# Block biases of a graph network leave the matmuls: one becomes a column, two are added to rows in SBUF by transfers from memory

## Chip, core and metric

One core of a Trainium2 chip. The time is that of one execution on the device in microseconds (us), and less is better. TensorE does the matrix products, VectorE and ScalarE take their results out of PSUM, GpSimd computes on SBUF alone, SyncE (SP) issues transfers. ScalarE and GpSimd can issue transfers too.

## What is computed

Four graph layers run over 512 nodes with 512 features, each `x = x + layer(relu(norm(x)))`, all in float32. The change touches mainly the second, a transformer of four blocks with attention along the edges (4 heads of 128):

```
for i in range(4):
    y = cond_norm(x, s1[i], b1[i])
    q, k, v = y @ wq[i] + bq[i], y @ wk[i] + bk[i], y @ wv[i] + bv[i]
    # per head: softmax of q.k over a node's edges, then the sum of p * v[dst]
    x = x + attention(q, k, v) @ wo[i] + bo[i]
    y = cond_norm(x, s2[i], b2[i])
    x = x + relu(y @ m_w1[i] + m_b1[i]) @ m_w2[i] + m_b2[i]
```

The first layer is a normalised adjacency product with two weights and biases, the third three diffusion steps, the fourth two relational layers of the form `agg + x @ root + bias`.

## The kernel before

Every product is made of three float32r matmuls, high by high, high by low and low by high part, so that a tile of 128 rows by 512 columns over 512 summed values takes 12 matmuls. A bias is a 13th matmul of the same shape: a selector (`sel`) times a tensor `brow` that holds the high and the low part of each bias in two rows. A tile goes to one of seven banks of PSUM (`ring`) in an order written out by hand (`l1_order`). ScalarE evicts the high part (`high`, L795), VectorE the low part (`low`, L1155, or L1157 with a column or a scalar). A bank is free again once the semaphore `tile_taken` has counted its eviction.

One block on TensorE (`attention_block`, L2013): transposes "Ta" of the normed rows `yp`; four tiles v; q and k per head; scores "s"; transposed probabilities "PT"; the mean value "PV" of a head, as columns `oT`; four tiles o = oT x wo, the first two begun before the last head is done; each o is added to the residual rows `xl` by VectorE (`residual`, L1544), which then takes the norm's statistics (`norm_stats`). GpSimd computes the inverse root (`inverse_root`, L695), VectorE the two halves of the conditioned norm (`conditioned`, L1487 and L1492) with two more tiles S and B. Transposes "Tb", the hidden tiles M, the tiles X, each added to `xl` again. Between X tiles the norm of the next block begins ("Sa", "Ba", then "Ta" 0).

Weights: ScalarE issues the load of a weight of 1 MB into one of three slots (L765) when the last user of the slot is done, rounds it to its high part (`high_weight`, L770), and GpSimd subtracts to get the low part (`low_weight`, L686). In a block the six weights are wv, wq, wk, wo, m_w1, m_w2 (j = 0 to 5; j = 6 is wv of the next block). GpSimd takes its work in the order of `block_lows` (L733): the splits of j = 1 to 4, four roots, the splits 5 and 6, four roots. ScalarE issues the load of j = 6 behind the eviction of the last "Tb" transpose.

SP loads `quad`, groups of the fourth layer's basis of 960 KB each, all through the kernel; TensorE mixes them (L1773) into a bank of their own. SP also loads the rows of the conditioning, the norms' biases (`load_cond`) and, once per block, the biases bv, bo, m_b1 and m_b2 into `braw` (`load_biases`); VectorE splits them into `brow` (`split_biases`) at the start of a block.

Of the kernel before, what the change touches and what calls it, by code (L numbers as in the profile page):

```python
# [14 lines left out]
P = 128  # L15
# [20 lines left out]
VECS = 5  # L36
COLUMN_BIASES = ("bq", "bk")
# [6 lines left out]
BASES = 30  # L44
VEC_ROWS = (VECS + len(COLUMN_BIASES) * BLOCKS) * KT

# [62 lines left out]
def program(nc, x_d, src_d, dst_d, type_d, w_d, noise_d, l0, l1, l2, l3, out_d, mix_d, ct_d, x_s):  # L109

    top = ExitStack()
    with top:
# [76 lines left out]
        bias_columns = sb("bias_columns", [P, len(COLUMN_BIASES), BLOCKS * KT])  # L189
        gate_e = mask[0:2, 0, :]  # L190
# [19 lines left out]
        braw = sb("braw", [P, D], ctx=cg)  # L210
        brow = sb("brow", [P, D], F32R, ctx=cg)
# [183 lines left out]
        braw_loaded = sem("braw_loaded")  # L395
        brow_hi = sem("brow_hi")
        brow_ready = sem("brow_ready")
# [71 lines left out]
        def _(sp):  # L469
# [25 lines left out]
            small(vec_rows[(VECS - 1) * KT:VECS * KT, :], l0["b_gcn"][0, :].rearrange("(k p) -> k p", p=P))  # L495
# [3 lines left out]
            vecs = [l0["b_mlp"][0:1], l0["b_gcn"][1:2], l0["b_mlp"][1:2]]  # L499
            vecs += [b.rearrange("(a d) -> a d", a=1) for b in (l2["b"], l3["bias"][0], l3["bias"][1])]  # L500
            for j, v in zip((0, 2, 3, 4, 5, 6), vecs):
                small(bias_raw[2 * j:2 * j + 2, :], v.broadcast_to([2, D]))
# [10 lines left out]
            def load_cond(b, n, ready):  # L513
                if ready is not None:
                    sp.wait_ge(cond_ready, ready)
                for k in range(2):
                    w_, b_ = l1[("s", "b")[k] + f"{n + 1}_w"], l1[("s", "b")[k] + f"{n + 1}_b"]
                    for g in range(3):
                        sp.dma_start(craw[32 * g:32 * g + COND, k, :],
                                     w_[bass.ds(b, 1)].rearrange("a c d -> (a c) d")).then_inc(cond_loaded, 16)  # L520
                    sp.dma_start(craw[96:98, k, :], b_[bass.ds(b, 1)].broadcast_to([2, D])).then_inc(cond_loaded, 16)

# [21 lines left out]
            def load_biases(i):  # L544
                for j, name in ((0, "bv"), (3, "bo"), (4, "m_b1"), (5, "m_b2")):
                    sp.dma_start(braw[2 * j:2 * j + 2, :], l1[name][bass.ds(i, 1)].broadcast_to([2, D])
                                 ).then_inc(braw_loaded, 16)

# [18 lines left out]
            load_biases(0)  # L567
# [4 lines left out]
            def block_loads(i, nxt, last):  # L572
# [8 lines left out]
                if not last:  # L581
                    sp.wait_ge(brow_ready, i + 1)
                    load_biases(nxt)
# [28 lines left out]
            store_set(SETS - 1)  # L612
            for t in range(NT):
# [6 lines left out]
        def _(pool):  # L620
# [25 lines left out]
            for clear in (bias_raw, fw2, cb, craw, braw, minus_low, minus_loww, quarter):  # L646
# [8 lines left out]
            for l in range(2):  # L655
                for r in range(2):
# [14 lines left out]
            g.affine_select(out=minus_loww[:], in_=minus_loww[:], compare_op=ALU.not_equal, fill=-1.0, base=-97,  # L671
                            pattern=[[0, 1]], channel_multiplier=1)

            g.iota(selv[:, 0, :, :], [[-2, 7], [0, P]], base=0, channel_multiplier=1, allow_small_or_imprecise_dtypes=True)
# [3 lines left out]
            pool.wait_ge(const_step, 6)  # L678
# [54 lines left out]
            def block_lows(i, last):  # L733
                for j in (2, 3, 4) if i == 0 else (1, 2, 3, 4):
# [3 lines left out]
                for j in (5, 6):  # L738
                    low_weight(i * 6 + (W1 + j), j % 3)
# [13 lines left out]
            for w in range(W3 + 2, W3 + 6):  # L753
# [4 lines left out]
        def _(act):  # L758
# [183 lines left out]
            for m in range(KT):  # L942
                high(n0, n0.base, ("U", m), hb_h[1][:, m, :])
# [20 lines left out]
            def block_highs(i, last, first=False):  # L964
# [46 lines left out]
                def mean_value(h):  # L1011
                    hi(("PV", h), oT_h[:, h, :])
# [120 lines left out]
        def _(dve):  # L1133
# [106 lines left out]
            def selectors():  # L1240
# [13 lines left out]
                v.tensor_copy(bg[:, :, 0:2], bias).then_inc(sel_step, 1)  # L1254
                v.tensor_copy(bias_columns[:], bank(n0, "vecs")[:, VECS * KT:VEC_ROWS].rearrange("p (j n) -> p j n", j=len(COLUMN_BIASES)))
# [48 lines left out]
            def split_cond(n, count):  # L1304

                dve.wait_ge(cond_loaded, count * 128 + 128)
# [145 lines left out]
            for m in range(KT):  # L1452
                low_of(("U", m), hb_l[1][:, m, :], hb_h[1][:, m, :])
# [9 lines left out]
            def split_biases(i):  # L1463

                dve.wait_ge(braw_loaded, i * 64 + 64)
                v.tensor_copy(brow[:], braw[:]).then_inc(brow_hi, 1)
                dve.wait_ge(brow_hi, i + 1)
                v.scalar_tensor_tensor(brow[:], f(brow[:]), minus_odd[:], braw[:], ALU.mult, ALU.add).then_inc(brow_ready, 1)

# [6 lines left out]

            split_biases(0)
# [40 lines left out]
            def attention_block(i, last, first=False):  # L1518
# [38 lines left out]
                def scaled(h):  # L1557
# [5 lines left out]
                    for j in range(NT):  # L1563
                        v.tensor_scalar(pr[:, j, :], pr[:, j, :], rden[:, h % 2, j:j + 1], hasedge[:, j:j + 1], ALU.mult, ALU.mult
                                        ).then_inc(probs_ready, 1)
# [11 lines left out]
                def mean_value(h):  # L1577
                    lo(("PV", h), oT_l[:, h, :], oT_h[:, h, :])
# [15 lines left out]
                else:  # L1594
                    transposed("a", 1)
                    split_biases(i)
# [110 lines left out]
            for l in range(2):  # L1707
# [10 lines left out]
                for t in range(NT):  # L1718
# [3 lines left out]
                    else:  # L1722
                        ready(n3, n3.base, name)
# [4 lines left out]
        def _(pe):  # L1728
# [256 lines left out]
            for m in range(KT):  # L1985
                tile0_by_rows(("U", m), bias_to_columns(2, bias_rows, m), wh[s], wl[s], m, hb_h[0], hb_l[0], lambda k: ("G", k))
# [26 lines left out]
            def attention_block(i, last, mixed_ahead=0):  # L2013
# [19 lines left out]
                def rows_product(name, t, lh, ll, w, bias):  # L2033
                    tile((name, t), [bias_to_rows(bias, brow)] + [p for k in range(KT) for p in
                         three(cols(lh, k, t), cols(ll, k, t), w[0][:, k, :], w[1][:, k, :])])

# [3 lines left out]

                def value_rows(t, w):
                    if t:
                        done(("Ta", t))
                    part(begin(T, b, ("v", t)),
                         [p for k in range(KT) for p in three(cols(yT_h, k, t), cols(yT_l, k, t), w[0][:, k, :], w[1][:, k, :])],
                         first=True)

                def value_bias(t):
                    if t == 0:
                        pe.wait_ge(brow_ready, i + 1)  # L2050
                    part(bank_of(("v", t)), [bias_to_rows(0, brow)], last=True).then_inc(tile_ready, 1)

                def value(t, w):
                    value_rows(t, w)
                    value_bias(t)
# [27 lines left out]
                def hidden(m, half, w):  # L2083
# [3 lines left out]
                    pairs = [(brow[:, m * P:(m + 1) * P], sel[:, 4:5, :].broadcast_to([P, NT // 2, P]))]  # L2087
# [22 lines left out]
                if i == 0:  # L2110
# [4 lines left out]
                    value_bias(0)  # L2115
# [4 lines left out]
                    value_bias(1)  # L2120
# [3 lines left out]
                    value_bias(2)  # L2124
# [45 lines left out]
                rows_product("o", 2, oT_h, oT_l, w, 3)  # L2170
                outs[3] = begin(T, b, ("o", 3))
                part(outs[3], [bias_to_rows(3, brow)] + head(3, 0) + head(3, 1) + head(3, 2), first=True)
# [19 lines left out]
                for t in range(NT):  # L2192
                    out = begin(T, b, ("X", t))
                    part(out, [bias_to_rows(5, brow)], first=True)
                    for k in range(KT):
                        if t == 0:
                            done(("M", k))
                        end = part(out, three(cols(vm_h, k, t), cols(vm_l, k, t), w[0][:, k, :], w[1][:, k, :]), last=k == KT - 1)
# [181 lines left out]
```

## Time and profile before

| | |
|---|---|
| median of 3 runs | 851.86 us (850.29 to 854.33) |
| the profiled execution | 849.76 us, its span 848.2 us |
| granted TensorE clock | 0.997 of full speed |
| TensorE matmuls | 823.0 us busy, 97% of the span, 4218 |
| weight loads into TensorE | 631.0 us, 74% |
| VectorE | 560.2 us, 66% |
| ScalarE | 395.1 us, 47% |
| GpSimd | 232.8 us, 27% |
| moved by transfers | 113.44 MB, 134 GB/s on average |

The busy time of an engine is a sum over its instructions, and matmuls overlap each other, so 97% says that TensorE nearly always has one under way, not how fast they follow each other. The blocks begin at about 215, 335, 451 and 567 us, and the fourth ends at 680 us.

### The profile page before, as it was taken

The numbers are of one execution on the slowest core, as the hardware profiler recorded it, in microseconds if no ns is written. First come the engines' busy times: TensorE is split into PE (matmuls) and PEld (weight loads), VectorE is DVE, ScalarE is ACT, GpSimd is POOL, SyncE is SP. The second block draws the span as 40 slices with busy tenths as digits, with TensorE's granted clock in tenths as the row PEclk, the third lists the DMA queues.
The fourth block names the chain that finished last, engine by engine and source line by source line (L and its number), as shares of the span: only waits on it lengthen the run. The fifth ranks groups of instructions, "written<-read, shape, count | busy, mean of one in ns | idle before, by whom it ended". The sixth has DMA issues, their size and how long they took to land.

```text
span 848.2 us, 13171 instructions
## 1 busy us (share of the span) xinstructions
PE 823.0 (97%) x4218; PEld 631.0 (74%) x4219; DVE 560.2 (66%) x1229; ACT 395.1 (47%) x646; POOL 232.8 (27%) x258
## 2 busy tenths in 40 slices
PE   5999979999899999999999999999999999999998
PEld 3666647777578788777797787887777967688786
DVE  7999998687887577477656666684767666720210
ACT  4999984444445513366223465134552244530200
POOL 4000024434512233411246022343112515422200
PEclk9999999999999999999999999999999999999999
DMA  9999965817442644653473646536436676030101
GB/s 186 202 218 226 269 159 144 198 63 177 124 122 57 185 102 143 157 114 112 96 202 101 146 88 178 125 130 153 104 118 157 186 212 181 13 100 1 49 13 38
DMA packets 59350, 113.44 MB, mean 134 GB/s; under 512 B 4372, under 2 KB 4936, under 8 KB 59292
## 3 DMA queue, kind: packets, MB, share of 16 engines
q1 hardware_dynamic: 42108, 79.00, 40.4%
q10 hardware_dynamic: 17184, 33.69, 12.1%
q8 instruction: 34, 0.56, 0.3%
q14 instruction: 24, 0.20, 0.1%
HBM read 105.33 MB, written 7.34 MB: 133 GB/s over the span
## 4 chain that ended last, share of the span: by engine, by line
PE 68%; DVE 2%; ACT 2%; DMA 1%; POOL 1%; issue 0%; DVEq 0%
PE ring L2030 24%; PE ring L1744 22%; PE ring L2339 5%; PE ring L1762 5%; PE mix_ps L1773 4%; PE ring L2326 3%; PE ring L2266 1%; PE ring L2267 1%; DMA wraw<-in_L_gnn_wv 1%; PE ring L2220 1%; PE ring L2221 1%; PE ring L2225 1%; PE ring L2297 1%; POOL wl L686 1%; ACT yp L988 0%
## 5 line engine op out<-in xcount | busy, mean ns | idle before, releaser
L686 POOL TENSOR_TENSOR wl<-wraw,wh 128x512 fp32r<-128x512 f32 x140 | 181.6, 1330 | 331.1 <-ACT wh L770 317.1
L695 POOL TENSOR_TENSOR rstd<-ve,half 128x1 f32<-128x1 f32 x48 | 26.4, 553 | 215.7 <-DVE ve L1173 215.4
L1846 PE MATMUL ring<-ohs,ohd 128*128 128x512 f32 x312 | 77.4, 399 | 2.8 <-DVE ohs L1345 2.8
L1846 PEld LDWEIGHTS ring<-ohs,ohd 128*128 128x128 f32 x312 | 57.4, 189 | 27.2 <-issue 14.8
L1323 DVE SCALAR_TENSOR_TENSOR ohd<-iota,dstT,vals 128x256 fp32r x156 | 69.6, 482 | 3.0 <-issue 1.8
L770 ACT ACTIVATE wh<-wraw 128x2048 fp32r<-128x2048 f32 x35 | 66.8, 1909 | 8.2 <-DMA wraw<-in_L_gnn_root 4.5
L795 ACT ACTIVATE yT_h<-ring 128x512 fp32r<-128x512 f32 x32 | 18.4, 598 | 99.4 <-PE ring L1762 99.4
L819 ACT ACTIVATE ohs<-iota,minus_srcT 128x512 fp32r<-128x512 f32 x78 | 52.2, 713 | 9.4 <-issue 6.5
L1744 PE MATMUL ring<-yT_h,wh 128*128 128x512 f32 x128 | 49.9, 390 | 1.2 <-DVE yT_l L1155 1.2
L1155 DVE TENSOR_TENSOR PT_l<-ring,PT_h 128x512 fp32r<-128x512 f32 x64 | 39.7, 682 | 16.4 <-ACT PT_h L795 16.4
L1744 PE MATMUL ring<-yT_h,wl 128*128 128x512 f32 x128 | 49.9, 389 | 0.0
L1744 PE MATMUL ring<-yT_l,wh 128*128 128x512 f32 x128 | 49.8, 389 | 0.0
L1773 PE MATMUL mix_ps<-quad,att_shift 120*32 120x512 f32 x384 | 46.8, 599 | 0.0
L795 ACT ACTIVATE qk_h<-ring,bias_columns 128x512 fp32r<-128x512 f32 x32 | 22.1, 690 | 52.6 <-PE ring L1744 52.6
L1157 DVE SCALAR_TENSOR_TENSOR qk_l<-ring,bias_columns,qk_h 128x512 fp32r<-128x512 f32 x32 | 23.6, 749 | 34.5 <-ACT qk_h L795 34.5
L823 ACT ACTIVATE ohs<-ohs 128x512 fp32r<-128x512 f32 x78 | 44.4, 617 | 0.0
L795 ACT ACTIVATE PT_h<-ring 128x512 fp32r<-128x512 f32 x64 | 33.0, 604 | 18.3 <-PE ring L1762 18.3
L795 ACT ACTIVATE vm_h<-ring 128x512 fp32r<-128x512 f32 x32 | 19.1, 596 | 47.4 <-PE ring L2030 47.4
L1345 DVE TENSOR_SCALAR ohs<-iota,srcT 128x512 fp32r<-128x512 f32 x78 | 38.0, 487 | 0.0
L2030 PE MATMUL ring<-yT_l,wh 128*128 128x256 f32 x128 | 36.2, 283 | 0.0
L2030 PE MATMUL ring<-yT_h,wl 128*128 128x256 f32 x128 | 36.2, 283 | 0.0
L2030 PE MATMUL ring<-yT_h,wh 128*128 128x256 f32 x128 | 36.2, 283 | 0.0
(389 smaller groups left out, 2135.2 us busy)
## 6 DMA issues: line engine op xcount, KB each, us to landing
quad<-in_L_gnn_basis SPq DMA_DIRECT2D x60, 960.0 KB, 11.0
wraw<-in_L_gnn_m_w ACTq DMA_DIRECT2D x8, 1024.0 KB, 6.6
mix_scratch<-mixed SPq DMA_DIRECT2D x128, 32.0 KB
wraw<-in_L_gnn_wv ACTq DMA_DIRECT2D x4, 1024.0 KB, 8.5
wraw<-in_L_gnn_wq ACTq DMA_DIRECT2D x4, 1024.0 KB, 5.3
wraw<-in_L_gnn_wk ACTq DMA_DIRECT2D x4, 1024.0 KB, 5.5
wraw<-in_L_gnn_wo ACTq DMA_DIRECT2D x4, 1024.0 KB, 5.2
wraw<-mix_scratch ACTq DMA_DIRECT2D x4, 1024.0 KB, 5.6
```

The lines of the kernel that those rows point to most:

```text
L686: last = g.tensor_tensor(wl[s][:, k, :], wraw[s][:, k, :], wh[s][:, k, :].bitcast(F32), ALU.subtract)
L770: a.activation(wh[s][:], wraw[s][:], ACT.Copy).then_inc(weight_hi, 1)
L795: a.activation(out, src, func, **kw).then_inc(hi_ready, 1)
L819: a.activation(ohs[:, s, :], iota[:], ACT.Abs, bias=minus_srcT[:, e]).then_inc(distance_ready, count)
L823: a.activation(ohs[:, s, :], ohs[:, s, :].bitcast(F32), ACT.Relu, bias=1.0, scale=-1.0).then_inc(src_ready, count)
L1323: return v.scalar_tensor_tensor(out, at.unsqueeze(1).broadcast_to([P, 4, HALF]), dstT[:, e], vals[:, e, :].rearrange("p a b -> p (a b)").u ...
L1744: last = te.matmul(out, l, r, start=n == 0, stop=n == len(pairs) - 1)
L1762: last = te.transpose(out[:, n * P:(n + 1) * P], ap, ident[:])
L1773: ins = te.matmul(mix_ps[c * STRIP:(c + 1) * STRIP, :], att_shift[0:QUADS * BASES, layer, GROUPS - 1 - k:GROUPS - 1 - k + STRIP], quad[0:Q ...
L1846: last = te.matmul(ring[:, banks[b], :], ohd[:, s, b, :], ohs[:, s, :], start=False, stop=False)
L2030: ins = te.matmul(out, l, r, start=first and n == 0, stop=last and n == len(pairs) - 1)
L2339: last = te.matmul(out, lhs, rhs, start=False, stop=r == 1 and t == NT - 1 and n == 2)
```

## The change

- bv leaves the v tiles. It becomes a column, added to "PV" by both evictions (`mean_value`). For that the mask of nodes without edges, `hasedge`, moves from the probabilities (`scaled`) to the o residual, which becomes `xl = o * hasedge + xl`.
- bo and m_b2 leave o and X. GpSimd issues transfers that add the bias row to all 128 partitions of `xl` (`add_rows`): bo to four tiles at once after the first norm of the block has read them (wait for "Ba" 3), m_b2 to tiles 0 and 1 after "Bb" 1 and to tiles 2 and 3 after "Bb" 3, both behind the four roots and ahead of the split of j = 5. VectorE's residuals wait for the transfers' semaphores.
- m_b1 stays on TensorE, read from two rows of `craw` and `cond` (row 100, `HIDDEN_ROW`); `braw`, `brow`, `load_biases` and `split_biases` go. `load_cond` issues nine transfers instead of eight.
- b_gcn of the first layer's second pass becomes a column, added to "U" by both evictions.
- The last bias of the fourth layer is loaded to 128 partitions of `quad`, and GpSimd adds it to `x` in four additions between the splits of W3+2 and W3+3.
- In v, the last of the twelve matmuls takes the place of the bias matmul (`value_end`).

```
             def block_lows(i, last):
-                for j in (2, 3, 4) if i == 0 else (1, 2, 3, 4):
+                def add_rows(name, tiles, done):
+                    rows_of = l1[name][bass.ds(i, 1)].unsqueeze(1).broadcast_to([P, len(tiles), D])
+                    g.dma_start(xl[:, tiles[0]:tiles[-1] + 1, :], rows_of, accum_op=ALU.add).then_inc(done, 16)
+
+                for j in (2,) if i == 0 else (1, 2):
+                    low_weight(i * 6 + (W1 + j), j % 3)
+                pool.wait_ge(tile_taken, b + T.at[("Ba", NT - 1)] + 1)
+                add_rows("bo", range(NT), output_biased)
+                for j in (3, 4):
                     low_weight(i * 6 + (W1 + j), j % 3)
                 for t in range(NT):
                     inverse_root(i * 8 + (12 + t), t)
-                for j in (5, 6):
-                    low_weight(i * 6 + (W1 + j), j % 3)
+                for j in range(2):
+                    pool.wait_ge(tile_taken, b + T.at[("Bb", 2 * j + 1)] + 1)
+                    add_rows("m_b2", range(2 * j, 2 * j + 2), hidden_biased[j])
+                low_weight(i * 6 + (W1 + 5), 5 % 3)
+                low_weight(i * 6 + (W1 + 6), 6 % 3)
...
-            for w in range(W3 + 2, W3 + 6):
+            low_weight(W3 + 2, slot(W3 + 2))
+            pool.wait_ge(end_bias_loaded, 16)
+            pool.wait_ge(y_ready, 2 * NT)
+            for t in range(NT):
+                g.tensor_tensor(x[:, t, :], x[:, t, :], quad[:, 0, 0, :], ALU.add).then_inc(end_biased, 1)
+            for w in range(W3 + 3, W3 + 6):
                 low_weight(w, slot(w))
...
                 def mean_value(h):
-                    hi(("PV", h), oT_h[:, h, :])
+                    hi(("PV", h), oT_h[:, h, :], ACT.Identity, bias=column_bias(2, h))
...
                 def residual(name, t):
+                    dve.wait_ge(hidden_biased[t // 2] if name == "X" else output_biased, i * 16 + 16)
                     ready(T, b, (name, t))
-                    v.tensor_tensor(xl[:, t, :], xl[:, t, :], bank(T, (name, t)), ALU.add).then_inc(tile_taken, 1)
+                    if name == "X":
+                        v.tensor_tensor(xl[:, t, :], xl[:, t, :], bank(T, (name, t)), ALU.add).then_inc(tile_taken, 1)
+                    else:
+                        v.scalar_tensor_tensor(xl[:, t, :], bank(T, (name, t)), hasedge[:, t:t + 1], xl[:, t, :], ALU.mult, ALU.add
+                                               ).then_inc(tile_taken, 1)
...
-                def value_bias(t):
-                    if t == 0:
-                        pe.wait_ge(brow_ready, i + 1)
-                    part(bank_of(("v", t)), [bias_to_rows(0, brow)], last=True).then_inc(tile_ready, 1)
+                def value_end(t, w):
+                    part(bank_of(("v", t)), value_pairs(t, w)[-1:], last=True).then_inc(tile_ready, 1)
...
-                    part(outs[t], [bias_to_rows(3, brow)] + head(t, 0) + head(t, 1), first=True)
+                    part(outs[t], head(t, 0) + head(t, 1), first=True)
...
-                    part(out, [bias_to_rows(5, brow)], first=True)
```

## Rows read from the trace of the kernel before

**Rows 1.** The chain that ended last, share by engine
```profile
PE 68%; DVE 2%; ACT 2%; DMA 1%; POOL 1%; issue 0%; DVEq 0%
```

**Rows 2.** Bias matmuls by tile: count, min/median/max ns, first and last start us
```profile
L2030 PE MATMUL ring<-brow,sel x44: 389/389/504, 221.9 to 677.4; 128*128 128x512 f32 x44
L1744 PE MATMUL ring<-brow,sel x4: 389/389/389, 298.1 to 645.3; 128*128 128x512 f32 x4
L1909 PE MATMUL ring<-sel,bias_rows x4: 389/476/481, 187.8 to 197.7; 128*128 128x512 f32 x4
L2326 PE MATMUL ring<-bias_rows,sel x4: 389/389/389, 811.2 to 836.3; 128*128 128x512 f32 x4
```

**Rows 3.** The chain in order of time, last layer: start us, us, what
```profile
755.63 5.44 PE ring L2339 x24
```

**Rows 4.** The chain where block 1 ends
```profile
429.23 9.51 DMA wraw<-in_L_gnn_wv
...
438.76 1.94 ACT wh L770
...
440.76 5.06 POOL wl L686 x4
...
446.37 0.76 DVE yp L1492
...
447.18 0.66 PE ring L1762 x4
```

**Rows 5.** Other boundaries: load issue, KB and us to landing, ScalarE, VectorE, TensorE
```profile
313.68 0.38 ACTq L765 DMA_DIRECT2D wraw<-in_L_gnn_wv  x1
...
wraw<-in_L_gnn_wv ACTq DMA_DIRECT2D x1, 1024.0 KB, 8.5
...
322.56 1.92 ACT L770 ACTIVATE wh<-wraw 128x2048 fp32r<-128x2048 f32 x1
...
330.26 0.75 DVE L1492 SCALAR_TENSOR_TENSOR yp<-yp,rstd,ring 128x512 f32<-128x512 f32 x1 [0.24 <-POOL rstd L695]
...
680.48 1.92 PE L1773 MATMUL mix_ps<-quad,att_shift 120*32 120x512 f32 x16
```

**Rows 6.** Evictions with and without a column: busy us, mean ns, idle before
```profile
L795 ACT ACTIVATE qk_h<-ring,bias_columns 128x512 fp32r<-128x512 f32 x32 | 22.1, 690 | 52.6 <-PE ring L1744 52.6
...
L795 ACT ACTIVATE oT_h<-ring 128x512 fp32r<-128x512 f32 x16 | 9.4, 586 | 9.9 <-PE ring L2030 9.7
...
L1157 DVE SCALAR_TENSOR_TENSOR qk_l<-ring,bias_columns,qk_h 128x512 fp32r<-128x512 f32 x32 | 23.6, 749 | 34.5 <-ACT qk_h L795 34.5
...
L1155 DVE TENSOR_TENSOR oT_l<-ring,oT_h 128x512 fp32r<-128x512 f32 x16 | 11.0, 687 | 7.4 <-ACT oT_h L795 7.4
```

**Rows 7.** Timeline of block 1 from its o tiles to X
```profile
412.24 0.69 DVE L1544 TENSOR_TENSOR xl<-xl,ring 128x512 f32<-128x512 f32 x1 [1.05 <-PE ring L2030]
...
425.44 5.03 POOL L686 TENSOR_TENSOR wl<-wraw,wh 128x512 fp32r<-128x512 f32 x4
...
425.61 0.75 DVE L1492 SCALAR_TENSOR_TENSOR yp<-yp,rstd,ring 128x512 f32<-128x512 f32 x1
...
436.94 0.40 PE L2030 MATMUL ring<-brow,sel 128*128 128x512 f32 x1
...
440.30 0.68 DVE L1544 TENSOR_TENSOR xl<-xl,ring 128x512 f32<-128x512 f32 x1
```

**Rows 8.** SP's issue; queues (packets, MB, share) in 430:431, then 319:320 (last row)
```profile
422.65 1.18 SPq L532 DMA_DIRECT2D quad<-in_L_gnn_basis  x2
...
q1 hardware_dynamic: 92, 0.19, 96.8%
q10 hardware_dynamic: 1, 0.00, 0.5%
...
q10 hardware_dynamic: 184, 0.37, 104.4%
```

**Rows 9.** GpSimd in the last layer
```profile
755.30 5.03 POOL L686 TENSOR_TENSOR wl<-wraw,wh 128x512 fp32r<-128x512 f32 x4 [21.34 <-ACT wh L770]
```

More of the change, by code:

```diff
@@ L394, in program @@
         cond_ready = sem("cond_ready")
-        braw_loaded = sem("braw_loaded")
-        brow_hi = sem("brow_hi")
-        brow_ready = sem("brow_ready")
+        output_biased = sem("output_biased")
+        hidden_biased = [sem(f"hidden_biased{j}") for j in range(2)]
+        end_bias_loaded = sem("end_bias_loaded")
+        end_biased = sem("end_biased")
         exp_ready = sem("exp_ready")
@@ L494, in _ @@
                     small(vec_rows[(l * 2 + r) * KT:(l * 2 + r + 1) * KT, :], l3["gate_w"][l][r, :, 0].rearrange("(k p) -> k p", p=P))
-            small(vec_rows[(VECS - 1) * KT:VECS * KT, :], l0["b_gcn"][0, :].rearrange("(k p) -> k p", p=P))
+            for l in range(2):
+                small(vec_rows[(4 + l) * KT:(5 + l) * KT, :], l0["b_gcn"][l, :].rearrange("(k p) -> k p", p=P))
             for j, name in enumerate(COLUMN_BIASES):
@@ L645, in _ @@
             pool.wait_ge(table_ready, 6)
-            for clear in (bias_raw, fw2, cb, craw, braw, minus_low, minus_loww, quarter):
+            for clear in (bias_raw, fw2, cb, craw, minus_low, minus_loww, quarter):
                 last = g.memset(clear[:], 0.0)
@@ L733, in block_lows @@
             def block_lows(i, last):
-                for j in (2, 3, 4) if i == 0 else (1, 2, 3, 4):
+                T = n1_last if last else n1 if i else n1_first
+                b = n1.base + i * PER
+                def add_rows(name, tiles, done):
[6 more added lines that the diff above has]
+                for j in (3, 4):
                     low_weight(i * 6 + (W1 + j), j % 3)
@@ L2039, in columns_product, with value_pairs @@
                          three(cols(w[0], k, m), cols(w[1], k, m), rh[:, k, :], rl[:, k, :])])
+                def value_pairs(t, w):
+                    return [p for k in range(KT) for p in three(cols(yT_h, k, t), cols(yT_l, k, t), w[0][:, k, :], w[1][:, k, :])]
                 def value_rows(t, w):
@@ L2169, in attention_block @@
                 condition(T, b, "b", 1, i * 2 + 2)
-                rows_product("o", 2, oT_h, oT_l, w, 3)
+                tile(("o", 2), [p for h in range(HEADS) for p in head(2, h)])
                 outs[3] = begin(T, b, ("o", 3))
-                part(outs[3], [bias_to_rows(3, brow)] + head(3, 0) + head(3, 1) + head(3, 2), first=True)
+                part(outs[3], head(3, 0) + head(3, 1) + head(3, 2), first=True)
                 transpose_rows(T, b, "b", 0)
@@ L2197, in attention_block @@
                             done(("M", k))
-                        end = part(out, three(cols(vm_h, k, t), cols(vm_l, k, t), w[0][:, k, :], w[1][:, k, :]), last=k == KT - 1)
+                        end = part(out, three(cols(vm_h, k, t), cols(vm_l, k, t), w[0][:, k, :], w[1][:, k, :]), first=k == 0, last=k == KT - 1)
                     end.then_inc(tile_ready, 1)
@@ L2322, in _ @@
                     else:
-                        pairs = [bias_to_rows(6, bias_rows)]
-                        pairs += [p for k in range(KT) for p in three(cols(h, k, m), cols(hl, k, m), wrh[:, k, :], wrl[:, k, :])]
+                        pairs = [p for k in range(KT) for p in three(cols(h, k, m), cols(hl, k, m), wrh[:, k, :], wrl[:, k, :])]
                     for n, (lhs, rhs) in enumerate(pairs):
```

75 lines of the change are left out of this document (32 added, 43 removed).

## Prediction

> **What bounds the kernel now.** I read the page's chain first: TensorE alone is 68% of it, and the rest of it is in small pieces [rows 1]. So a matmul that goes is worth time if nothing else is waiting at that place. The second view is the groups of the bias matmuls [rows 2]: they are shown as 389 ns or more each, but this is the length of one, not its step. In the chain 24 matmuls of the same shape take 5.44 us [rows 3], 0.2267 us each, because the next starts while the last one drains. The price of a removed 512-column matmul is therefore 0.2267 us, not 0.39; who multiplies by the length predicts 22 us instead of 13. The third view is the chain where one block meets the next [rows 4, 5]. There TensorE isn't the bound alone: the weight wv of the next block is loaded, rounded by ScalarE, split by GpSimd, and only then does GpSimd compute the root that the next norm needs.
>
> **What goes.** In each of four blocks 4 tiles of v, 4 of o and 4 of X lose a bias matmul: 48 (the trace has 44 + 4 records). U loses 4 and the last layer's R loses 4 [rows 2]. 56 x 0.2267 = **12.7 us**, the gross gain. The hidden layer keeps its 32; they only read another tensor.
>
> **What of it is lost on the way.**
> (a) First block, v. The pieces of v stand between transposes that wait for VectorE. The last of the twelve matmuls now stands where the bias stood, so for v0 and v1 the shorter part lies ahead of a wait. Lost: nothing at best, 4 x 0.23 = 0.9 at worst; I take 0.4.
> (b) Head 3's mean value gets its column added by both evictions. With a column ScalarE takes 690 ns instead of 586, VectorE 749 instead of 687 [rows 6], and o's last part waits for exactly this: 0.16 us, four times: 0.6 (0 to 0.7).
> (c) The o residual takes the form with a scalar: 0.07 us more than the 0.68 of the plain one (the row at 440.30 in [rows 7]; 749 in [rows 6]), twice ahead of the transpose of tile 1, which TensorE reaches 0.45 us sooner: 0.1 a block, 0.4 (0 to 0.6).
> (d) The block boundary. In block 1 the wv load is issued when the last transpose of the second norm is evicted (429.23) and lands after 9.51 us; ScalarE 438.76, GpSimd 440.76 for 5.06 us, the norm's second half 446.37, and TensorE, waiting, transposes at 447.18 [rows 4]. The start of this chain moves with TensorE, its length does not. Between the two TensorE sheds three X biases, 0.68 us: all of it is waited for here. After blocks 0 and 2 VectorE waited 0.24 us for the root [rows 5] and TensorE not at all, so 0.2 is to spare and 0.48 lost. Together 1.6 (0 to 2.0).
> 12.7 - 0.4 - 0.6 - 0.4 - 1.6 = **9.7 us**.
>
> **What is added: the transfers.** bo is a transfer of 1 MB per block that reads the rows in SBUF, adds and writes them. It starts once the opening norms have read them, behind GpSimd's second weight of the block. From the boundary at 330.26 [rows 5] to the first o residual at 412.24 [rows 7] are 82 us: hidden, unless it takes ten times what any load of this size does. m_b2 is two transfers of 0.5 MB with far less room. GpSimd issues them behind the four roots at 425.4, the second once the fourth tile is normalised (425.61 + 0.75 = 426.4), and then splits the next weight, 5.03 us, which so far began at 425.44. It is due when X begins at 436.94, the first sum is due at 440.30 [rows 7]. So with issues that cost nothing the split ends at 431.4, with 5.5 us to spare, and the first transfer has 14 us. No row of before shows an accumulating transfer, its issue by GpSimd or its wait; the issue I bound by nothing and by 1.2 us for two of SP's [rows 8] each, which the 5.5 us cover twice. Queued behind this GpSimd wait are only the two splits and the next roots.
>
> The price is what these transfers do to the wv load. At 422.65 SP has issued two loads of the basis [rows 8], and they fill the engines: in 430 to 431 the SP queue holds 96.8% of them and the wv load, issued at 429.23, 0.5%. Its 1 MB then moves at 0.37 MB in 1 us, 2.8 us in all. That is, a transfer waits for those that stand whole in front of it. Let d be the delay of wv's landing. The first m_b2 transfer is ready before the second basis load's turn is over, or even before it begins, and goes ahead of wv; the second comes about when wv does. One 0.5 MB transfer at the wv load's own rate is 1.4 us; reading the destination as well makes 2.8 at most by that rate; both transfers ahead of wv, at this double cost, are 5.6. No delay at all is also possible, if both go behind wv. I take **d = 1.5**: one transfer, plain rate, that being the nearest row.
>
> The Trainium skill (DMA: Bandwidth & Descriptors, Queues, rings and completion order) says that an engine takes its queues in turn and drains a whole packet, which it puts at some tens of descriptors at most, before it switches. This agrees with 96.8% against 0.5%. If one took turns by single rows of 2 KB instead, wv would have had half of the engines in that microsecond, and all of both transfers would stand between its packets, d near the upper end.
>
> What d costs: in block 1 all of it. After blocks 0 and 2 wv lands at 313.68 + 8.5 = 322.2 and ScalarE takes it at 322.56, in its order [rows 5]: 0.4 is free, d - 0.4 each. In block 3 the load is layer 2's weight; I take the same 0.4 as free, and 1.0 more, since TensorE has 1.92 us of mixing there between X and what waits for the roots [rows 5]: d - 1.4. The sum is 4d - 2.2 from 1.4 on: 3.8 us at 1.5.
>
> **Nearly free.** The bias rows of the last layer: GpSimd was idle for 21.34 us ahead of a split of four such operations in 5.03 us [rows 9]; four additions more fit in. If they didn't, the split of W3+3 would be late by them. SP issues one small load more for each norm and four fewer per block, and it mostly waits. VectorE loses the split of the bias rows, some 1.2 us a block, at a place where TensorE is busy with v0 and v1: no gain. The scale of the probabilities with one scalar instead of two, and the column on U: the evictions have idle time in front of them.
>
> **Sum.** 9.7 - 3.8 = 5.9 us less. The profiled execution took 849.76 us with a span of 848.2; 849.76 - 5.9 = 843.9. The median of the runs shown is 851.86, 2.1 above it (0.25%), so on the median: **846.0 us**, 0.7% faster.
>
> The change in general is 4d - 11.9 for d of 1.4 and more: -4.3 at d = 1.9, nothing at 3.0, +4.3 at 4.05, +10.5 at 5.6. 4.3 us, 0.5%, is about what a measurement of this kernel can tell from no change (its three runs lie 4 us apart).
>
> **The rivals.**
> 1. *No delay* (d = 0): the second basis load keeps its turn, wv follows it, the additions come last. For it: in-order service as seen at 430 us. Against it: the first addition is issued 4 us before wv. 851.9 - 9.7 = 842.2 us.
> 2. *The additions are dear to wv* (this one ends on the other side). Both go ahead of wv, or one costs much more than a load because each of its 256 rows per transfer reads SBUF, adds, and fetches the same 2 KB of memory. Place: the end of each block, the wait of ScalarE for wv. From d = 3.0 the gain is gone; at 5.6 it is 862 us. For it: the engines are full in just this stretch, and the block 1 chain has no slack. Against it: only one of the two has a clear lead on wv. Its lighter half, d of 2 to 4, is "no change", about 852.
> 3. *The sum itself is late.* VectorE's first X residual waits for the transfer instead of the matmul. It decides from 14 us after the issue; at 20 us each block would stand for 6: 846 + 24 = 870 us. Against it: twice that size, wv, lands after 9.51 us with the engines full [rows 4].
> 4. *GpSimd is late.* If each issue holds it for over 2.7 us, the split of m_w2 ends after 436.94 and TensorE stands before X; at 5 us each, 4.5 a block and 864 us. For it: no row shows what this issue takes. The Trainium skill (SBUF — State Buffer, SBUF: two separate sides) says that GpSimd writes the descriptors of its transfers itself, and can't while VectorE runs in its two-port mode. Here VectorE is on evictions and norms with an operand in PSUM at 425 to 430, so little would change.
> 5. *The gain is smaller than the count*: VectorE paces o and X once TensorE is shorter, and half of the 9.7 goes. 849 to 852, no change.
>
> **Chances.** Forecast (d from 0.7 to 1.9) 0.34; rival 1 0.21; rival 2 0.27, of it 0.15 no change and 0.12 slower; rival 3 0.05 and rival 4 0.03, slower; rival 5 0.10, no change. Faster by over 0.5%: 0.34 + 0.21 = 0.55. Within: 0.25. Slower: 0.20. The range: from rival 1 with (a) to (d) at their better ends (841) to where rival 2 is nearly whole, 858. The forecast alone: 843.5 to 848.
>
> **What the profile after would show.** TensorE with 56 matmuls less; the step of 0.2267 us unchanged. The wv load of block 1 landing 11 us after its issue, not 9.51, ScalarE's wait for it grown, and TensorE idle by 1 to 3 us before the transposes at each of three boundaries, where it now has 0.04. No wait of VectorE for the transfers, and GpSimd's split of m_w2 done before X. I am wrong if the wv load lands as before (rival 1), if it takes 13 us and more (rival 2), or if VectorE's residual or TensorE's first X matmul waits for a DMA or for GpSimd (rivals 3, 4).

## The result, and the profile after

The changed kernel takes **875.86 us** (median of 4 runs, 873.69 to 882.97) against 853.10 for the kernel before beside it (4 runs): a ratio of 1.0293, 95% interval 1.0259 to 1.0327. It is 22.8 us slower. The prediction said 846.0 (841 to 858), 5.9 us faster. Rival 2, the additions dear to wv, ended on the right side, but its worst case, 862 us, is still 14 us short.

The profiled execution is the slowest of the four, 882.97 us against 849.76 before. It also begins 4 us late: ScalarE rounds the weight wq of block 0 at 210.40 instead of 206.41, and that point is uneven even among the kernels below that are the same as the changed one up to there (204.8 to 209.3). So I compare stretches inside the trace.

The page of the changed kernel, its queues (packets, MB, share of 16 engines), the chain by engine, and three loads (KB, us to landing):

```profile
PE 825.2 (94%) x4162; PEld 630.3 (72%) x4163; DVE 554.0 (63%) x1222; ACT 397.7 (45%) x646; POOL 250.4 (28%) x276
...
q0 software_dynamic: 4288, 8.39, 5.4%
...
PE 72%; DMA 12%; DVE 6%; ACT 4%; POOL 3%; SPq 2%; issue 1%; ACTq 0%; DVEq 0%
...
wraw<-in_L_gnn_wv ACTq DMA_DIRECT2D x4, 1024.0 KB, 14.1
...
xl<-in_L_gnn_bo POOLq DMA_DIRECT2D x4, 1024.0 KB, 12.3
```

The 56 matmuls are gone (4218 to 4162). A new queue moves 8.39 MB. Transfers are 12% of the chain, but this can't be set against the 1% in [rows 1]: that chain reaches back to 215 us only, this one to the start. Behind 215 us transfers are 84.0 us of the changed kernel's chain and 9.5 us of the kernel before's. Not all of it is loss, since the chain of `no_additions` below has 48.9 us there. wv lands after 14.1 us; 8.5 was the median before [rows 5]. Where TensorE waited from 200 to 700 us, by what released it (us in total, times, longest):

```profile
PE ring L1779 <- DVE yp L1504: 18.1, 5, 5.8
PE ring L2047 <- DVE yT_l L1175: 5.3, 4, 1.7
PE ring L1761 <- DVE qk_l L1177: 4.6, 1, 4.6
```

16.7 us of the first line are three waits of 5.58, 5.78 and 5.32 us, at the ends of blocks 0, 1 and 2. The kernel before had 0.30 us at the end of block 1 and none at the other two. The chain of the changed kernel where block 1 ends, in order of time, answers to [rows 4]:

```profile
445.12 14.47 DMA wraw<-in_L_gnn_wv
...
459.61 1.93 ACT wh L790
...
461.61 4.93 POOL wl L687 x4
466.54 0.53 POOL rstd L696
...
467.10 0.76 DVE yp L1504
...
467.90 1.11 PE ring L1779 x4
469.01 4.41 PE ring L2047 x12
```

It is the chain of before, link for link, with 4.96 us more in its first link (14.47 against 9.51). The last line is new in kind: 12 matmuls of an X tile take 4.41 us, where 12 such matmuls take 2.76 in `transfers_order` below. In block 0 the same stretch by windows (busy us of PE, PEld, DVE, ACT, POOL with counts, then the granted clock, DMA share, GB/s):

```profile
342.00:346.00 4.00, 0.92 (x5) 0.93 (x6) 1.69 (x3) 0.00 (x0) 2.76 (x4) 0.59 0.00 0
346.00:350.00 4.00, 4.00 (x12) 3.13 (x12) 2.70 (x7) 0.60 (x1) 0.55 (x1) 0.55 0.00 0
350.00:354.00 4.00, 4.00 (x21) 3.29 (x20) 3.11 (x8) 2.40 (x2) 1.02 (x2) 1.00 0.39 92
```

TensorE was idle for 5.58 us, and then worked near the lower of its two levels (0.5 of full speed is 1.2 GHz) for most of 4 us. Against 2.76 us, the X tile behind the stall is 1.6 us longer in blocks 0 and 1 (4.38 and 4.41) and 1.1 us longer in block 2 (3.81).

The third wait is in block 0. The chain of the changed kernel there:

```profile
250.15 6.78 DMA craw<-in_L_gnn_m_b
256.95 0.70 DVE cond L1328
257.68 1.29 DVE cond L1330
258.96 1.33 DVE qk_l L1177 x2
...
260.34 1.69 PE ring L1761 x4
```

VectorE stands in `split_cond(0, 2)`, waiting for the rows that SP loads, and behind it in its order are the evictions of q and k of head 1, for which TensorE waits. In 238 to 262 us GpSimd's queue, with bo, holds 31.4% of the transfer engines. The last of these rows lands 6.78 us after its issue; in `no_additions` below it takes 3.63. Here too TensorE is slow behind its wait: the 12 matmuls from 260.34 on take 4.61 us against 3.01 there, and the granted clock is 0.50 in 262 to 264 us.

### The profile page after: what moved, and what is told of

It is laid out like the page before. It is cut to its first block, busy times and chain, and to the rows that moved or that the text cites. A ratio compares the mean times of both kernels' runs of the same rounds, so it can differ in the third digit from the quotient of the medians.

```text
span 881.1 us, 13102 instructions
## 1 busy us (share of the span) xinstructions
PE 825.2 (94%) x4162; PEld 630.3 (72%) x4163; DVE 554.0 (63%) x1222; ACT 397.7 (45%) x646; POOL 250.4 (28%) x276
## 3 DMA queue, kind: packets, MB, share of 16 engines
q0 software_dynamic: 4288, 8.39, 5.4%
## 4 chain that ended last, share of the span: by engine, by line
PE 72%; DMA 12%; DVE 6%; ACT 4%; POOL 3%; SPq 2%; issue 1%; ACTq 0%; DVEq 0%
PE ring L1761 19%; PE ring L2047 14%; PE ring L1863 6%; PE ring L1931 5%; PE ring L2349 5%; PE ring L1779 5%; DMA wraw<-in_L_gnn_wv 5%; PE mix_ps L1790 4%; PE ring L2336 3%; DMA quad<-in_L_gnn_basis 2%; POOL wl L687 2%; DMA wraw<-in_L_gnn_wk 2%; DMA wraw<-in_L_gnn_W 2%; ACT wh L790 2%; PE mix_ps L1881 1%; PE ring L2277 1%
## 5 line engine op out<-in xcount | busy, mean ns | idle before, releaser
L1863 PEld LDWEIGHTS ring<-ohs,ohd 128*128 128x128 f32 x312 | 58.0, 191 | 26.1 <-issue 13.6
L1779 PE MATMUL ring<-ident,yp 128*128 128x128 f32 x256 | 35.2, 281 | 18.2 <-DVE yp L1504 18.1
L1779 PEld LDWEIGHTS ring<-ident,yp 128*128 128x128 f32 x256 | 29.9, 144 | 25.4 <-DVE yp L1504 20.8
L1504 DVE SCALAR_TENSOR_TENSOR yp<-yp,rstd,ring 128x512 f32<-128x512 f32 x32 | 23.9, 747 | 20.4 <-POOL rstd L696 17.5
## 6 DMA issues: line engine op xcount, KB each, us to landing
wraw<-in_L_gnn_wv ACTq DMA_DIRECT2D x4, 1024.0 KB, 14.1
```

The costliest lines, as they stand in the source:

```text
L1779: last = te.transpose(out[:, n * P:(n + 1) * P], ap, ident[:])
L1863: last = te.matmul(ring[:, banks[b], :], ohd[:, s, b, :], ohs[:, s, :], start=False, stop=False)
```

## Experiments

The column "us" has medians, beside the median of the kernel before on the same chip; "profiled" is the one execution that was traced. The column "stretch" goes from the start of ScalarE's rounding of block 0's wq to that of the second weight behind block 3, in the profiled execution; it leaves the uneven start and the last layer out. Where the profiled execution lies far from the median (by 3 us and more: changed, plain_m_b2, gpsimd_adds, gpsimd_order), its stretch is no measure of the median.

| kernel | us | before there | ratio, 95% | profiled | stretch |
|---|---|---|---|---|---|
| before | | | | 849.76 | 492.8 |
| changed | 875.86 | 853.10 | 1.0259 to 1.0327 | 882.97 | 522.5 |
| no_additions | 848.61 | 851.67 | 0.9944 to 0.9973 | 848.15 | 489.8 |
| no_m_b2 | 855.05 | 851.67 | 1.0013 to 1.0045 | 855.77 | 496.4 |
| no_bo | 871.56 | 851.67 | 1.0211 to 1.0261 | 869.51 | 514.3 |
| half_m_b2 | 864.73 | 851.67 | 1.0121 to 1.0183 | 864.68 | 505.6 |
| plain_m_b2 | 872.34 | 852.30 | 1.0215 to 1.0251 | 866.07 | 510.7 |
| early_wv | 854.19 | 852.30 | 1.0004 to 1.0033 | 854.39 | 495.8 |
| gpsimd_adds | 853.55 | 852.30 | 0.9993 to 1.0037 | 858.17 | 491.8 |
| gpsimd_order | 849.36 | 852.30 | 0.9949 to 0.9980 | 846.24 | 486.4 |
| transfers_order | 844.11 | 851.86 | 0.9892 to 0.9933 | 843.63 | 485.6 |
| no_additions_order | 842.84 | 851.86 | 0.9878 to 0.9918 | 840.35 | 485.4 |
| before_order | 851.47 | 851.86 | 0.9979 to 1.0012 | 851.47 | 492.3 |
| before_no_m_b2 | 850.79 | 851.86 | 0.9968 to 1.0004 | 851.24 | 491.9 |

### Which transfer costs what

Four kernels take transfers out of the changed kernel. The waits for them go too.

```
no_additions, no_bo:
-                pool.wait_ge(tile_taken, b + T.at[("Ba", NT - 1)] + 1)
-                add_rows("bo", range(NT), output_biased)
no_additions, no_m_b2:
-                for j in range(2):
-                    pool.wait_ge(tile_taken, b + T.at[("Bb", 2 * j + 1)] + 1)
-                    add_rows("m_b2", range(2 * j, 2 * j + 2), hidden_biased[j])
half_m_b2:
-                for j in range(2):
+                for j in range(1):
```

> The changed kernel without the transfers that add bo and m_b2, so both biases are missing from its result; the rest of the change stands. Theory A (the transfers are the whole loss, through what they delay): wv lands about 9 us after its issue again, no wait of VectorE for craw in block 0, TensorE idle under 2 us at a boundary; before minus 9.7 to 11.3 us, 842 to 844 us. Theory B (a good part of the loss is in the rest of the change: columns in the evictions, the masked residual, the ninth load of the conditioning, the slower start): 848 us or more.

> The changed kernel without the two m_b2 transfers of a block; m_b2 is missing from its result, bo is still added. Theory A1 (m_b2 is the dear one since it meets the wv load with full engines; bo costs only the 4.6 us wait for craw in block 0): wv lands after 9 us, 842 to 844 plus 4.6, 847 to 849 us. Theory A2 (both transfers are dear, bo through wo, m_w1 and the basis loads too): 853 us or more.

> The changed kernel without the bo transfer; bo is missing from its result, m_b2 is still added. Theory A1: the 4.6 us wait of VectorE for craw in block 0 goes, the boundaries stay as they are (wv landing 14 us, TensorE idle over 5 us): 876 minus 4.6, 870 to 872 us. Theory A2: 866 us or less. If the wait for craw stays, it was not bo that held the craw load.

> The changed kernel with only the first of the two m_b2 transfers of a block (tiles 0 and 1); tiles 2 and 3 miss m_b2. Theory A (delay in proportion to what is moved, both go ahead of or beside wv): wv landing near 11.5 us instead of 14, about half of the 28 us between no m_b2 and both comes back, 860 to 864 us. Rival (only the first, issued 4 us ahead of wv, delays it; the second comes too late): wv still lands after 13 us or more and the time stays within 3 us of 876. Rival (the delay starts with the second): under 852.

Measured: 848.6, 855.1, 871.6 and 864.7 us. The first was expected from 842 to 844 by theory A and 848 or more by B: **B**. Without these transfers the change is worth 3.1 us, not 9.7. From there bo costs 6.4, and m_b2 another 20.8 on top of bo (875.9 less 855.1); taking bo out of the changed kernel gives 4.3 back. So m_b2 is the dear one. By its number no_m_b2 fell to A2: its base was 848.6 and not 843, and bo costs 6.4 and not 4.6. What speaks against A2 is no_bo, 871.6 where A2 had 866 or less. There TensorE's wait for qk_l in block 0 falls from 4.6 us to 1.2, and the waits at the ends of the blocks stay. Of bo's price, 5.2 us lie between the roundings of wk and wo in block 0 (43.09 us in no_m_b2, 37.88 in no_additions): the rows of the conditioning land 3.4 us later after their issue (7.02 against 3.63), and the 12 matmuls behind the wait take 4.51 us against 3.01, at a granted clock of 0.50 in 260 to 262 us. half_m_b2 stands near the middle, 9.7 and 11.1 us from its two neighbours, 0.7 us above A's range. The delay of wv in block 1 goes with it. The first link of the chain there in no_m_b2, then in half_m_b2:

```profile
435.97 9.51 DMA wraw<-in_L_gnn_wv
```

```profile
440.13 11.52 DMA wraw<-in_L_gnn_wv
```

So d is 2.0 with one transfer and 5.0 with both: 9.51, 11.52, 14.47 us to landing. Both go beside wv; the second isn't too late for it, and the first isn't ahead of it. In 447 to 448 us of the changed kernel, some 6 us after the first was issued, GpSimd's queue has 6.8% of the engines and SP's 99.7%. Then wv and both additions run side by side. The queues in 452 to 453 us of the changed kernel, and in 435 to 436 us of the kernel before, each 6 to 7 us after the issue of wv:

```profile
q0 software_dynamic: 65, 0.11, 62.1%
q10 hardware_dynamic: 77, 0.16, 45.1%
```

```profile
q10 hardware_dynamic: 146, 0.30, 94.8%
```

### Is it the adding?

```
plain_m_b2:
-                    add_rows("m_b2", range(2 * j, 2 * j + 2), hidden_biased[j])
+                    rows_of = l1["m_b2"][bass.ds(i, 1)].unsqueeze(1).broadcast_to([P, 2, D])
+                    g.dma_start((unused_rows[:], qk_h[:])[j], (rows_of, rows_of.bitcast(F32R))[j]).then_inc(hidden_biased[j], 16)
```

> The changed kernel, but the two m_b2 transfers of a block only write the same rows, of the same size, issued by GpSimd at the same places, to memory that nobody reads; m_b2 is missing from the result. Theory A (an accumulating row costs the engines about twice a plain one, as 68.3% against 33.9% for equal bytes showed): the delay of wv halves, landing near 11 to 12 us, and half of the 21 us between no m_b2 (855.05) and the changed kernel comes back: 862 to 867 us. Theory B (what costs is that GpSimd's queue takes turns with the wv queue, adding or not): within 3 us of 876.

The median is 872.3: 3.5 us below the changed kernel, outside A's 862 to 867, just outside B's 3 us. But its profiled execution took 866.07 us, the other four 869.65 to 873.31, and in these the granted clock is lower (0.982 in the second, where the profiled one has 0.990). In the profiled one wv lands after 12.12 us in block 1, so d = 2.6, half of 5.0, as A had it. The queues in comparable stretches, first 327 to 330 us of the changed kernel, then 324 to 327 of plain_m_b2 (packets, MB, share of 16 engines):

```profile
q0 software_dynamic: 192, 0.38, 68.3%
q10 hardware_dynamic: 169, 0.35, 33.9%
```

```profile
q0 software_dynamic: 211, 0.49, 52.9%
q10 hardware_dynamic: 200, 0.41, 44.2%
```

q0 is GpSimd's queue, q10 ScalarE's with wv. Byte for byte, an accumulating row holds the engines for 1.8 times as long as a loaded one (68.3 / 0.38 against 33.9 / 0.35); a plain row from the same queue costs what wv's do (52.9 / 0.49 against 44.2 / 0.41). All queues together moved 0.77 MB in the first 3 us and 0.99 in the second, with the engines full in both. And in both kernels the two queues run side by side. So both parts of the cost are seen in the traces: the sharing, and the higher price of adding. How the 20.8 us of the medians divide between them is not settled. By the medians plain transfers give back only 3.5 us. By the stretches it is 11.8 of 26.1, but there the slowest execution of one kernel stands beside the fastest of the other, and the clock behind the stalls differs from execution to execution.

### Is it only the landing of wv?

```
early_wv:
                 for r in range(NT):
                     norm_rows("b", r)
-                lwi(6, after(("o", NT - 1)))
+                    if r == 1:
+                        lwi(6, after(("o", NT - 1)))
```

> The changed kernel with all its transfers; ScalarE issues the wv load (j = 6) behind the second Tb eviction instead of the fourth, some 8 us earlier and so ahead of both m_b2 transfers. Theory A (m_b2 costs only through the landing of wv, which is what the end of the block waits for): most of the 21 us of m_b2 comes back, less what wk's load is still late: 857 to 862 us, TensorE idle under 2 us ahead of the boundary's transposes. Theory B (the additions are slow for themselves: they now share with wv and the X residual waits, or wk is as late as before): 866 us or more, with VectorE waiting for xl or for wk.

854.2 us: 21.7 less than the changed kernel, with every byte of the transfers still moved, and better than A's 857 to 862. wv lands after 5.4 us (median), the m_b2 transfers after 13.1, and VectorE waits for none of them. That is level with no_m_b2 (855.1), which doesn't have these transfers: what they cost is the landing of wv. What is left against no_additions, 5.6 us, is bo: the 4.8 us wait of TensorE for qk_l in block 0 is still there.

### Where does the gain of the matmuls go?

```
before_no_m_b2 (on the kernel before; the first of the twelve matmuls now opens the sum):
-                    part(out, [bias_to_rows(5, brow)], first=True)
...
before_order (on the kernel before), gpsimd_order, no_additions_order, transfers_order: as early_wv, and
+                    lwi(2, b)
                     norm_rows("a", 1)
-                    lwi(2, b)
...
-                low_weight(i * 6 + (W1 + 6), 6 % 3)
+                if last:
+                    low_weight(i * 6 + (W1 + 6), 6 % 3)
                 for t in range(NT):
+                    if not last and t < 3:
+                        low_part(i * 6 + (W1 + 6), 0, ((0, 1), (2,), (3,))[t])
```

> The kernel before without the 16 bias matmuls of X (m_b2 is missing from the result), nothing else changed. By the count: 16 x 0.2267 = 3.6 us less. Theory A (what TensorE sheds among the X tiles it waits for at the block's end, where the chain of wv sets the time): 0.2 to 1.5 us less, mostly in the last block; TensorE waits for yp by up to 0.7 us at each boundary. Theory B (by the count): 3 us less or more.

> The kernel before, biases on TensorE, with the same three moves at the block's end. Theory A (TensorE had cover there: it waited 0.04 to 0.24 us, so a shorter chain is worth nothing without fewer matmuls): within 1 us of before. Theory B (the moves carry the gain of gpsimd_order by themselves): 3 us below before or more.

> Both additions left out (bo and m_b2 are missing from the result), with the three moves at the block's end alone. What the removed matmuls are worth once the chains at the boundary are shorter: theory A 848.6 - 5.7 = 841 to 844 us; theory B (the gain is eaten elsewhere) 846 to 848 us.

before_no_m_b2 is 1.1 us faster, not 3.6, and its interval doesn't tell it from no change at all. Its trace says where: from the rounding of wq in block 0 (208.86) to that of layer 2's weight (672.18) it needs 463.3 us, as the kernel before does (206.41 to 669.74, 463.3). Twelve matmuls gone there bought nothing. From there to the next weight (700.78, before 699.25) it is 0.9 us shorter, the four matmuls of the last block. TensorE's waits from 300 to 700 us, in the kernel before and then in before_no_m_b2:

```profile
PE ring L1762 <- issue: 0.7, 3, 0.2
...
PE ring L1762 <- DVE yp L1492: 0.3, 1, 0.3
```

```profile
PE ring L1762 <- DVE yp L1492: 1.9, 3, 0.9
PE ring L1762 <- issue: 1.4, 3, 0.5
```

The moves alone, before_order, are worth nothing that can be told (851.5 against 851.9). With the bias matmuls gone, and bo and m_b2 not added at all, they are worth 5.8 us (842.8 against 848.6). Both expectations of theory A held: a shorter chain and fewer matmuls are worth something only together. The chain of no_additions shows the second eater behind the first:

```profile
429.84 9.48 DMA wraw<-in_L_gnn_wv
...
441.34 5.04 POOL wl L687 x4
446.38 0.52 POOL rstd L696
...
452.29 5.86 DMA wraw<-in_L_gnn_wk
...
458.18 1.92 ACT wh L785
```

wk is loaded into the slot of m_w2, so it can't be issued before the last X tile is done; it lands, ScalarE rounds it, and behind that stands the eviction of v for which VectorE and then TensorE wait. In this execution TensorE waited 0.20, 0.56 and 0.90 us for yT_l at blocks 1, 2 and 3. From the rounding of wq to that of wo, where v sheds 0.91 us, no_additions is shorter than the kernel before by 0.63 us in block 1, 0.22 in block 2 and not at all (-0.07) in block 3. So what TensorE sheds in X goes into the wait for wv, and of what it sheds in v the most goes into the wait for wk.

### Two ways out

In `gpsimd_adds` SP loads both bias rows to all partitions, and GpSimd adds them. `gpsimd_order` is the same with the three moves.

```
gpsimd_adds:
+                def add_rows(j, last_read):
+                    pool.wait_ge(rows_loaded, i * 32 + 32)
+                    pool.wait_ge(tile_taken, b + T.at[last_read] + 1)
+                    for t in range(NT):
+                        g.tensor_tensor(xl[:, t, :], xl[:, t, :], added_rows[:, j, :], ALU.add).then_inc(rows_added, 1)
...
+                add_rows(0, ("Ba", NT - 1))
...
                 low_weight(i * 6 + (W1 + 5), 5 % 3)
+                add_rows(1, ("Bb", NT - 1))
```

> The changed kernel without accumulating transfers, nothing left out: SP loads bo and m_b2 to all partitions (0.25 MB each, plain), and GpSimd adds them to xl, four operations of some 1.3 us for bo behind the split of j = 2, four for m_b2 behind the split of j = 5, where it is idle until wv is rounded. Theory A (the arithmetic is free there): as with both additions left out, 848.6, so 847 to 850 us. Theory B (GpSimd's splits of wo or wv come late, or GpSimd and VectorE slow each other): 852 us or more.

> As gpsimd_adds, and three moves at the block's end: wv's load issued behind the second Tb eviction, wk's load ahead of the eviction of Ta 1 (1.1 us earlier), and the roots of tiles 0 and 1 between the pieces of wv's split instead of behind it (1.0 us earlier). Theory A (the gain of the removed matmuls is eaten at the block's end, where the chain wv, split, root, norm and then the chain of wk don't get shorter with TensorE): some 2 us at each of three boundaries come back, 841 to 845 us. Theory B (the gain is lost elsewhere, VectorE pacing o): no more than 1 us below gpsimd_adds.

853.6 us (850.86 to 859.95) and 849.4. The first missed: 5 us above no_additions instead of level with it. The second is above A's 841 to 845, but 4.2 us below gpsimd_adds where B allowed 1; its stretch, 486.4, is within 1 us of those of transfers_order and no_additions_order. The arithmetic fits where it was meant to. GpSimd in block 1 of gpsimd_adds:

```profile
436.01 5.04 POOL L696 TENSOR_TENSOR wl<-wraw,wh 128x512 fp32r<-128x512 f32 x4
441.01 5.04 POOL L751 TENSOR_TENSOR xl<-xl,added_rows 128x512 f32<-128x512 f32 x4
```

Its stretch is only 2.0 us longer than that of no_additions. The rest lies ahead of it: the profiled execution began 8 us later than that of no_additions (216.21 against 208.39), and its runs scatter by 9 us. SP's two loads for block 0 stand ahead of that point; but gpsimd_order has the same loads and began at 209.71. Why the start is so uneven I did not find.

transfers_order keeps the accumulating transfers, with the three moves above and a fourth, bo's issue behind the split of j = 3 instead of j = 2:

```
-                for j in (2,) if i == 0 else (1, 2):
+                for j in (2, 3) if i == 0 else (1, 2, 3):
                     low_weight(i * 6 + (W1 + j), j % 3)
...
-                for j in (3, 4):
+                for j in (4,):
```

> The changed kernel whole, with its accumulating transfers, and four moves: wv's load ahead of m_b2 (as in early_wv), wk's load ahead of the eviction of Ta 1, two roots between the pieces of wv's split, and the bo transfer issued behind the split of j = 3 instead of j = 2, some 20 us later in block 0, so that it no longer lies on the small craw loads. Theory A (bo costs the 4.8 us wait for craw in block 0; the rest of the loss is the chains at the block's end): 854.2 - 4.8 - 4 (three boundaries at 1.3 to 2 each) = 844 to 847 us. Theory B (bo delays whatever is loaded beside it, now m_w1 and later the o residual waits): 849 us or more.

**844.1 us**, 0.9% faster than the kernel before and 3.6% faster than the changed one, and 1.3 us above no_additions_order, which leaves bo and m_b2 out. The end of block 1 in its chain:

```profile
428.54 13.37 PE ring L2051 x89
...
442.38 2.75 PE ring L2051 x12
...
446.07 2.76 PE ring L2051 x12
448.83 0.48 issue
449.32 0.63 PE ring L1783 x4
449.94 0.93 PE ring L1765 x4
450.87 5.46 PE ring L2051 x24
```

No transfer stands in it, and an X tile's 12 matmuls take 2.76 us. wv is issued at 420.07, 5.05 us ahead of the first m_b2. In block 0 wo is rounded at 263.37, where early_wv had 269.41: nothing else lies in between but bo's later issue and the 0.5 us by which this execution is ahead. VectorE's wait for the rows of the conditioning there is 0.4 us, where early_wv had 4.4.

## Why the prediction was wrong

**The step that failed first is (d)'s price, "I take d = 1.5: one transfer, plain rate".** d was 5.0 at block 1. The bound that the same paragraph worked out, both transfers at double cost, 5.6, was nearly the truth; the nearest row misled. It took one transfer at the price of a plain load. One adding transfer alone gave 2.0 (half_m_b2), two plain ones 2.6 (plain_m_b2), two adding ones 5.0: both the number and the price were short. Neither went ahead of wv as the step had it; both shared the engines with it. Two things were against that row: the queues of the rows at 430 to 431 us are both called hardware queues, and GpSimd's is another kind (q0, software); and nothing there adds. That the row says how GpSimd's queue stands to ScalarE's was an assumption. By the prediction's own sum, 4d - 11.9 at 5.0 is 8.1 us slower; the rest is in the two steps below and in what stands behind a stall.

**The second is the 9.7 us that were to be kept.** Here no_additions measured 3.1. Rival 5 had it as "half of the 9.7 goes", and for the reason that VectorE paces o and X. At o half of it goes: from the rounding of m_w1 in block 1 to the eviction of the last "Tb" transpose the kernel before takes 29.03 us and the changed one 28.60, 0.43 for 0.91 shed. The first two of the four matmuls are kept whole (10.15 and 9.69 us from the rounding of m_w1 to that of m_w2); the last two buy nothing. Steps (b) and (c) had 0.26 of this loss a block. That VectorE's chain of residual, statistics and norm sets the time there is what the changed kernel's chain shows in block 1; no run took it out. The larger part is the block's end: in (d) I counted X's 0.68 as lost but let v's four matmuls through, and did not follow the chain of wk, which takes them. before_no_m_b2 shows the X part by itself.

**The third is bo, "hidden, unless it takes ten times what any load of this size does".** The transfer was in time for its reader. It was dear to others: the 4 KB and 32 KB rows of the conditioning that were issued behind it, for which VectorE stood in its order in block 0, and TensorE behind it. 6.4 us by the medians. I had looked only at who waits for bo, not at who shares the engines with it, though I had done just that for m_b2.

These three, -3.1, 6.4 and 20.8 for m_b2, sum by construction to 24.2 us, the changed kernel against the 851.67 of these experiments (22.8 against its own 853.10). Taken in the other order bo is 4.3 and m_b2 23.0 (871.56 less 848.61), so each is known to about 2 us. The 20.8 is 3.0 more than the prediction's own 4d - 2.2 = 17.8 at d = 5.0. In the profiled executions, whose stretches are 26.1 us apart, 18.7 lie in the four later landings of wv and layer 2's weight (5.4, 5.0, 4.3 and 4.2), and 7.6 behind the first three, up to the rounding of wo. No step had these: the X tile at the lower clock, 1.6, 1.6 and 1.1 us, and wk, which lands after 6.7 us against 5.9.

What held: the step of 0.2267 us and the 56 matmuls; no wait of VectorE for either sum (rival 3), though closely, since the first m_b2 transfer of block 1, issued at 441.67, landed after 13.7 us at 455.4 and the residual began at 456.16; GpSimd in time (rival 4), with 1.21 us an issue, about the 1.2 a piece that was taken; the additions of the last layer's bias in GpSimd's idle time, of which 9.48 us were left. The sign to look for was named: "if it takes 13 us and more (rival 2)".

The Trainium skill (DMA: Bandwidth & Descriptors, Queues, rings and completion order) has each engine take its queues in turn, a whole packet at a time; the prediction added that turns by single rows would put d near the upper end. In 327 to 330 us of the changed kernel q0 and q10 move 192 and 169 packets side by side, so the trace agrees with turns between these two queues, whatever their length; it was the upper end. The row that the prediction took as agreement, 96.8% against 0.5% in 430 to 431 us, shows no turns: two queues with work that take turns would share. There wv had been issued 0.8 us before, and it stayed under 9% until 433 us. Whether its rows were ready in that time no run shows.

## What to carry over

- A transfer that its reader never waits for can still be the dearest part of a change. List what is issued within its landing time behind and beside it, small loads too, and ask which of them ends a wait; then issue the one that matters first. Moving one issue of 0.4 us ahead by 8.5 us was worth 21.7 us here.
- A chain of load, rounding, split and root does not get shorter because the engine at its end has less to do. Matmuls removed ahead of its end are worth little until the chain is shortened too, and shortening it alone is worth nothing either: 3.1 us for all the matmuls, 0.4 for the moves (no change that can be told), 9.0 for both, with bo and m_b2 left out of the first and the last.

## What the runs showed of the hardware

- A transfer that adds into SBUF holds the engines about 1.8 times as long, byte for byte, as a load (68.3% for 0.38 MB against 33.9% for 0.35 MB in the same 3 us). Its issue takes GpSimd 1.21 us for 256 rows; that of a plain one of 256 rows 0.73 to 0.79 us (plain_m_b2).
- GpSimd's queue and ScalarE's shared the engines: 192 packets beside 169 in 327 to 330 us. Beside SP's basis load both got less: in 324 to 327 us SP's queue had 80.9% of the engines, GpSimd's 26.7% and ScalarE's wv load 0.4%, and in 447 to 448 us SP's had 99.7%, GpSimd's 6.8% and ScalarE's nothing. (The shares can sum to more than 100%.)
- After an idle time of 5.58 us TensorE's granted clock was 0.55 in 346 to 350 us, after one of 4.6 us 0.50 in 262 to 264 us; both are near or at its lower level. After one of 0.69 us in no_additions it was 1.00, and the 12 matmuls took 2.77 us.
